# A four-layer graph network on one core: the fourth layer's neighbour weights applied before the sums

## The reference

```
h  = relu(layernorm(x));  x1 = x + log_softmax(sage(relu(sage(h))))        # layers 1 and 2
h  = relu(layernorm(x1)); h  = relu(mean(h)@W_l0.T + b_l0 + h@W_r0.T)      # layer 3: 128 -> 256
h  = relu(mean(h)@W_l1.T + b_l1 + h@W_r1.T)                                # layer 4: 256 -> 256
out = x1 + relu(h@W_lin1.T + b_lin1) @ W_lin2.T + b_lin2
```

## Time and profile before

| | |
|---|---|
| median of 3 runs | 591.04 us (590.75 to 591.55) |
| time of the profiled execution | 590.59 us |
| its span in the profile | 588.7 us |
| TensorE busy, matmuls / weight loads | 545.3 us (93%) / 291.9 us (50%) |
| VectorE, ScalarE, GpSimd busy | 223.0, 204.5, 24.0 us |
| granted TensorE clock, mean | 0.998 of full |
| DMA traffic | 29.47 MB, mean 50 GB/s |

### The profile page before, as it was taken

The page is one execution under the profiler, slowest core; times in us unless marked ns, Lnnn a source line. Parts: engine busy times, 40 slices in busy tenths (PEclk is TensorE's granted clock), DMA queues, the critical chain, the costliest instruction groups (busy, mean ns, idle before and its releaser), DMA issues.

```text
span 588.7 us, 9420 instructions
## 1 busy us (share of the span) xinstructions
PE 545.3 (93%) x3078; PEld 291.9 (50%) x3078; DVE 223.0 (38%) x496; ACT 204.5 (35%) x370; POOL 24.0 (4%) x34
## 2 busy tenths in 40 slices
PE   1356999999999999999999999999999999999996
PEld 0234655555554554445455555544545445454555
DVE  6788977586765316667511110100000001010001
ACT  1588867576774313545522221200001010100011
POOL 4320000000000000010100000000000000000000
PEclk9999999999999999999999999999999999999999
DMA  3700103010000134232131111241011211111011
GB/s 93 193 3 1 28 10 116 2 36 17 17 18 17 23 70 126 80 96 79 28 88 53 49 48 44 61 124 52 13 40 36 52 35 52 35 35 52 15 34 29
DMA packets 31372, 29.47 MB, mean 50 GB/s; under 512 B 4894, under 2 KB 30879, under 8 KB 31215
## 3 DMA queue, kind: packets, MB, share of 16 engines
q1 hardware_dynamic: 29622, 27.91, 17.1%
q10 hardware_dynamic: 1561, 0.84, 0.6%
q0 software_dynamic: 160, 0.33, 0.3%
HBM read 19.68 MB, written 9.39 MB: 49 GB/s over the span
## 4 chain that ended last, share of the span: by engine, by line
PE 86%; DVE 5%; ACT 3%; DMA 3%; issue 2%; POOL 1%; ACTq 0%; DVEq 0%; SPq 0%; POOLq 0%
PE ps L1025 54%; PE ps L1042 22%; PE ps L979 5%; PE ps L1297 2%; DVE hs_b L491 1%; DMA adj<-key_d,adj 1%; PE ps L1035 1%; ACT hs_b L796 1%; PE ps L1259 1%; ACT adj L1488 1%; DMA invc<-inv_d 1%; PE ps L1231 1%; DMA adj<-in_dst_dram 1%; POOL adj L1371 1%; DVE adj L1415 1%
## 5 line engine op out<-in xcount | busy, mean ns | idle before, releaser
L1025 PE MATMUL ps<-adj,hs_b 125*128 (+2 forms) x1050 | 203.6, 351 | 0.0
L1025 PE MATMUL ps<-adj,hs_a 125*128 (+2 forms) x700 | 158.4, 353 | 0.0
L1025 PEld LDWEIGHTS ps<-adj,hs_b 125*128 125x128 f16 x1050 | 96.3, 97 | 103.9 <-issue 6.6
L491 DVE TENSOR_TENSOR hs_b<-iota,hs_b 128x1024 f16<-128x1024 f16 x150 | 96.0, 688 | 29.4 <-PE ps L979 27.7
L979 PE MATMUL ps<-hs_b 128*128 128x125 f16 x625 | 69.4, 235 | 21.4 <-DVE hs_b L491 13.4
L835 ACT ACTIVATE adj<-ps 125x500 f32 (+2 forms) x150 | 80.2, 543 | 23.5 <-PE ps L979 17.0
L979 PEld LDWEIGHTS ps<-hs_b 128*128 128x128 f16 x625 | 46.7, 104 | 67.1 <-DVE hs_b L491 35.0
L1025 PEld LDWEIGHTS ps<-adj,hs_a 125*128 125x128 f16 x700 | 58.5, 97 | 38.7 <-issue 5.2
L964 ACT ACTIVATE actT<-ps,col 128x500 f32<-128x500 f32 (+1 forms) x14 | 8.9, 633 | 148.0 <-PE ps L1042 148.0
L785 DVE TENSOR_TENSOR hs_a<-ps,hs_a 125x512 f32<-125x512 f32 (+1 forms) x7 | 4.4, 635 | 128.5 <-PE ps L1297 128.5
L1042 PE MATMUL ps<-aggT,wts 128*128 128x500 f32 (+1 forms) x112 | 44.6, 540 | 0.4 <-ACT aggT L946 0.4
(11 more groups left out here) (149 smaller groups left out, 355.1 us busy)
## 6 DMA issues: line engine op xcount, KB each, us to landing
invc<-inv_d SPq DMA_DIRECT2D x24, 250.0 KB, 3.3
h_d<-actT SPq DMA_DIRECT2D x6, 500.0 KB, 3.1
wts<-h_d SPq DMA_DIRECT2D x6, 500.0 KB, 4.0
self_d<-hs_b SPq DMA_DIRECT2D x6, 250.0 KB, 2.0
hs_b<-self_d SPq DMA_DIRECT2D x6, 250.0 KB, 3.5
hs_b<-in_x_dram SPq DMA_DIRECT2D x6, 250.0 KB
x_d<-hs_b SPq DMA_DIRECT2D x6, 250.0 KB
hs_a<-x_d SPq DMA_DIRECT2D x6, 250.0 KB
```

The lines of the kernel that those rows point to most:

```text
L491: last = nc.vector.tensor_tensor(onehots[slot], iota2.unsqueeze(1).to_broadcast(shape), keys[:, ds(g * 4, 4), :].unsqueeze(2).to_broadcast ...
L1025: last = nc.tensor.matmul(acc[:, 0:n], hs[:, ds(s * (2 * w) + part * w + h * 128, 128)], adj[0:P, ds(c * (S * C) + s * n, n)], start=(isin ...
```

## The change

The rows of layer 4's input are multiplied by `Wl1` node by node before they are summed. `project3` takes the place of `turn3`: the block of `actT` that was transposed is now the stationary operand, and a 256 column half of `Wl1` moves. `own_term3` computes `Wr1` times the activations in layer 3; ScalarE adds the bias and sends that to DRAM (`v_d`) instead of the activations. In layer 4 `hidden4` is gone: VectorE scales the sum, adds `v`, and ScalarE applies the ReLU. As the projected rows need a scale, a bound is computed: four one-column matmuls in layer 2, step 1 (`bound_sums`), a small matmul (`bound_row`) in the last step, and on VectorE `projected_bound` and `projected_scale`, the latter ahead of layer 2's last `step2`. Two 256 KB weight loads are issued at the entry of layer 2. The branch for graphs that don't fit (`slow`) is changed alike and isn't run here. The diff, cut to its core:

```diff
@@ SyncE
             sp.wait_ge(sem("p1_low"), NCH)
             spread(2, hbz[:, 0:S * 2 * D], D, hs_d2)
+            sp.dma_start(wts[:, 512:1024], wt_d[:, 512:1024]).then_inc(sem("w1_in"), 16)
+            sp.dma_start(zT[:, 0:512], wt_d[:, 1024:1536]).then_inc(sem("w1_in"), 16)
...
-                sp.wait_ge(sem("p3_relu"), 2 * c + 2)
-                sp.dma_start(h3_d[:, :, ds(c * C, n)],
+                elif not slow:
+                    load_fourth()
+                n = width(full)
+                sp.wait_ge(sem("p3_vT"), 2 * c + 2)
+                sp.dma_start(v_d[:, :, ds(c * C, n)],
...
+            def load_fourth():
+                sp.wait_ge(sem("p3_agg_out"), NCH)
+                sp.wait_ge(sem("p3_own"), NCH)
+                sp.dma_start(w4, wt_d[:, 1536:2304]).then_inc(sem("w4_in"), 16)
+                load_inv("p4_", 0, True)
+                load_x1(0, True)
...
-                    sp.wait_ge(sem("p4_h4"), 2 * c + 2)
-                    load_h3(c + 1, nxt)
+                    sp.wait_ge(sem("p4_pre"), 2 * c + 2)
+                    load_v(c + 1, nxt)
@@ VectorE
+            def projected_bound():
+                dve.wait_ge(sem("u_bound"), 1)
+                lk(nc.vector.tensor_reduce(ubound, bank(6, 2), AX, ALU.max))
+                nc.vector.tensor_scalar(actT[:, 512:640], identf[:], 0.0, ubound, ALU.mult, ALU.add).then_inc(sem("u_spread"), 1)
+            def projected_scale():
+                dve.wait_ge(sem("u_bound"), 2)
+                lk(nc.vector.tensor_reduce(ubound, bank(0, 128), AX, ALU.max))
+                lk(nc.vector.tensor_scalar(ubound, ubound, TOP, None, ALU.mult))
+                pow2(lk, us, ius, ubound)
+                dve.sem_inc(sem("u_spread"), 1)
             step2(1, True)
+            projected_bound()
             with dve.Fori(2, NFULL) as c:
                 step2(c, True)
+            if not slow:
+                projected_scale()
             step2(NFULL, False)
...
-                    nc.vector.tensor_tensor(aggT[:, h * C:h * C + n], bank(h, n), invc[:, 0:n], ALU.mult).then_inc(
+                    nc.vector.scalar_tensor_tensor(o4, bank(h, n), ius, invc[:, 0:n], ALU.mult, ALU.mult).then_inc(
                         sem("p4_agg_out"), 1)
+                    dve.wait_ge(sem("p4_v"), 16 * c + 16)
+                    nc.vector.tensor_tensor(o4, o4, wts[:, h * C:h * C + n], ALU.add).then_inc(sem("p4_pre"), 1)
@@ ScalarE
+            act.wait_ge(sem("w1_in"), 32)
+            nc.scalar.activation(actT[:, 0:512], wts[:, 512:1024], ACT.Abs).then_inc(sem("abs_l1"), 1)
             chunks(act, step2)
...
+            def relu3(c, full):
+                wait_past(act, "p3_v_out", 16 * c)
...
+            def own_term(c, full):
+                act.wait_ge(sem("p3_v"), 2 * c + 2)
+                for m in range(2):
+                    nc.scalar.activation(actT[:, m * C:m * C + n], bank(4 + m, n), ACT.Identity,
+                                         bias=bl1c[:, m:m + 1]).then_inc(sem("p3_vT"), 1)
+            def step3(c, full):
+                high3(c - 1, True)
+                own_turned(c, full)
+                own_term(c - 1, True)
+                relu3(c, full)
@@ TensorE
+            def bound_sums():
+                for m in range(2):
+                    for k in range(2):
+                        last = nc.tensor.matmul(bank(6)[:, m:m + 1], actT[:, k * 256 + m * 128:k * 256 + m * 128 + 128], ones_c,
+                                                start=(k == 0), stop=(k == 1))
+            def bound_row():
+                nc.tensor.matmul(bank(0, 128), actT[:, 512:640], identf[:], start=True, stop=True)
+                   once=((1, 14, bound_sums), (NFULL, 12, bound_row)))
...
-                wait_past(pe, "p3_relu", 2 * c)
+                wait_past(pe, "p3_vT", 2 * c)
-            def turn3(c, full):
+            def project3(c, full):
                 pe.wait_ge(sem("p3_relu"), 2 * c + 2)
                 wait_past(pe, "p3_low", 2 * c)
...
-                            last = nc.tensor.transpose(bank(6 + k, 4 * D, P)[:, at:at + 128],
-                                                       actT[:, m * C + t * P:m * C + (t + 1) * P], identf[:])
+                            last = nc.tensor.matmul(bank(6 + k, 2 * H, P)[:, (t - t0) * H:(t - t0 + 1) * H],
+                                                    actT[:, m * C + t * P:m * C + (t + 1) * P], l1v[:, m, :],
+                                                    start=(m == 0), stop=(m == 1))
+            def own_term3(c, full):
+                pe.wait_ge(sem("p3_relu"), 2 * c + 2)
+                for m in range(2):
+                    dense(4 + m, n, [(r1v[:, k, m * 128:m * 128 + 128], actT[:, k * C:k * C + n]) for k in range(2)])
-            staged(3, [(lambda c: bank(acc3(c, slow)), ha, D, 0)], [(0, own3, 1), (8, hidden3, 1), (0, turn3, 2)],
+            staged(3, [(lambda c: bank(acc3(c, slow)), ha, D, 0)], [(0, own3, 1), (8, hidden3, 1), (0, project3, 2), (4, own_term3, 2)],
...
-                   [(10, hidden4, 1), (20, lin1, 1), (30, lin2, 1)],
-                   [(0, own3, NFULL), (0, turn3, NFULL - 1), (8, hidden3, NFULL), (16, turn3, NFULL)],
+                   [(7, lin1, 1), (17, lin2, 1)],
+                   [(0, own3, NFULL), (0, project3, NFULL - 1), (4, own_term3, NFULL - 1), (9, hidden3, NFULL),
+                    (15, project3, NFULL), (19, own_term3, NFULL)],
-                for part in (hidden4, lin1, lin2):
+                for part in (lin1, lin2):
                     part(NFULL, False)
```

More of the change, by code:

```diff
@@ L198, in sage_program @@
         mv = over(hs_b, up + 10368, 4 * 2, F32)[0:P]
[L200 removed]
+        w4 = over(hs_a, 0, 768, F32)
         x1in = over(hs_a, 7168, 4 * D, F32)[0:P]
@@ L432, in phase @@
                 if slow:
-                    pool.wait_ge(sem(f"p{ph}_rows"), 16)
+                    pool.wait_ge(sem("rows"), 16 * ph)
                 def step(c, full):
@@ L1154, in pe_layers @@
                 pe.wait_ge(sem("absw"), 2)
-                pe.wait_ge(sem("p1_rows"), 16)
+                pe.wait_ge(sem("rows"), 16)
                 chunks(pe, slow1)
@@ L1163, in pe_layers, with staged @@
                 step1(NFULL, False, None)
-            def staged(ph, aggs, parts, lead, source, fill=(0, 0)):
+            def staged(ph, aggs, parts, lead, source, fill=(0, 0), once=()):
                 def slow_step(c, full):
@@ L1212, in step @@
                                 part(c - lag, True)
+                        for of, tiles_done, part in once:
+                            if isinstance(c, int) and c == of and at == tiles_done:
+                                part()
                         if at % S == 0 and ph > 2 and at >= done:
@@ L1232, in turn2 @@
                 last.then_inc(sem("p2_turned"), 1)
+            def bound_sums():
+                pe.wait_ge(sem("abs_l1"), 1)
+                for m in range(2):
+                    for k in range(2):
+                        last = nc.tensor.matmul(bank(6)[:, m:m + 1], actT[:, k * 256 + m * 128:k * 256 + m * 128 + 128], ones_c,
+                                                start=(k == 0), stop=(k == 1))
+                last.then_inc(sem("u_bound"), 1)
+            def bound_row():
+                pe.wait_ge(sem("u_spread"), 1)
+                nc.tensor.matmul(bank(0, 128), actT[:, 512:640], identf[:], start=True, stop=True).then_inc(sem("u_bound"), 1)
+            if slow:
+                bound_sums()
             staged(2, [(each_own, hbz, D, 0)], [(7, turn2, 1)],
-                   [(0, own1, NFULL), (6, hidden1, NFULL), (12, second1, NFULL), (17, turn1, NFULL)], (NFULL - 1, NFULL, NCH))
+                   [(0, own1, NFULL), (6, hidden1, NFULL), (12, second1, NFULL), (17, turn1, NFULL)], (NFULL - 1, NFULL, NCH),
+                   once=((1, 14, bound_sums), (NFULL, 12, bound_row)))
+            if slow:
+                bound_row()
             pe.wait_ge(sem("w0_in"), 16)
@@ new lines, in project3 @@
+                    last.then_inc(sem("p3_u"), 1)
+            def own_term3(c, full):
+                n = width(full)
+                pe.wait_ge(sem("p3_relu"), 2 * c + 2)
+                for m in range(2):
+                    dense(4 + m, n, [(r1v[:, k, m * 128:m * 128 + 128], actT[:, k * C:k * C + n]) for k in range(2)]).then_inc(
+                        sem("p3_v"), 1)
+            staged(3, [(lambda c: bank(acc3(c, slow)), ha, D, 0)], [(0, own3, 1), (8, hidden3, 1), (0, project3, 2), (4, own_term3, 2)],
+                   [(14, turn2, NFULL)], (NFULL - 1, NFULL, NCH), fill=(5, 8))
@@ L1273, in hidden4, with lin1 @@
+            av = w4[:, 0:512].rearrange("p (k o) -> p k o", k=2)
+            bv = w4[:, 512:768].rearrange("p (k o) -> p k o", k=2)
+            def lin1(c, full):
                 n = width(full)
                 pe.wait_ge(sem("w4_in"), 16)
-                pe.wait_ge(sem("p4_h3"), 16 * c + 16)
-                pe.wait_ge(sem("p4_agg_out"), 2 * c + 2)
```

(7 more changed lines are left out.)

88 lines of the change are left out of this document (46 added, 42 removed).

## The result

The changed kernel takes **593.42 us** (591.80 to 594.82, 10 runs), the kernel before 590.76 (590.34 to 591.55, 10 runs). The ratio is 1.0044, with a 95% interval of 1.0033 to 1.0055, so 2.7 us more. The profiled execution took 594.35 with a span of 592.4 us, 3.7 more than before's 588.7.

A forecast was written before the change was run, and what follows sets the result against it. TensorE, 86% of the ending chain, was taken as the bound. Terms -5.3 + 0.2 + 0.6 + 1.75 - 0.15 + 1.1 + 0.9 + 1.45 + 0.2 = +0.75 us took the median from 591.04 to 591.8, range 589.6 to 594.4.

The forecast's parts named there:

- Full steps: Layers 3 and 4: steps of 21.2 us instead of 15.3, and 26.2 instead of 32.95.
- Rival B: Layer 3: `hidden3` waits in each step because ScalarE starts two evictions late; 593.6 us, chance 0.10.
- Matmul work: TensorE in layers 3 and 4: 47.8 us removed, 42.5 added, net -5.3 us.
- Rival D: Layer 3's projection: a 256 column instruction is paced by its weights, 0.233 us; 593.5 us, chance 0.07.
- Rival E: Layer 3: each removed transpose frees its recorded 0.279 us, 14.0 instead of 5.8; 583.6 us, chance 0.02.
- Short steps: Last steps of layers 3 and 4: chunk 5's `hidden3` +0.6 net, `lin1` +1.75, last `lin1` -0.15, v +0.2 us.
- The bound: Layer 2: one-column matmuls on TensorE +0.9 us, `projected_scale` on VectorE +1.45 us.
- The entry: Start of layer 2: two weight loads ahead of the inverse degrees cost +1.1 us, bounds 0 and 2.4.
- the two readings: Entry of layer 2: inverse degrees 0.6 us late, own term behind them 1.3 us late.
- the line: DMA landing time at layer 2's entry: 256 KB in 2.8 us, 896 KB in 5.8, 4.7 ns per KB.
- Rival A: Entry of layer 2: weight loads delay the inverse degrees by 2.4 us instead of 1.1; 593.1 us, chance 0.18.
- C: Entry of layer 2: the weight loads cost nothing, as x's data are the slow part; 590.7 us, chance 0.17.

The follow-up runs named there:

- the loads alone: Kernel before plus only the two weight loads at the entry of layer 2, data unused: 593.29 us, ratio 1.0039.
- loads early: Changed kernel with the two weight loads issued earlier, ahead of the entry of layer 2: 592.10 us, ratio 1.0018 to the kernel before.
- sums early: Changed kernel with the eight one-column matmuls ahead of tile 6 instead of tile 14 in layer 2: 592.43 us, ratio 1.0026 to the kernel before.
- no bound: Changed kernel with scale set to 1, bound computation left out, weight loads behind the entry's three loads: 589.71 us, ratio 0.9984 to the kernel before.
- all places: Changed kernel with weight loads and one-column matmuls earlier, scale last, `lin1` and `lin2` later, x1 load before output write: 588.48 us, ratio 0.9965 to kernel before.
- all in place: Changed kernel with all five placements mended, plus the short chunk's last sum written over its x1 rows: 588.54 us, ratio 0.9961 to the kernel before.
- the loads behind: Changed kernel with the two weight loads issued behind the three loads of layer 2's entry: 592.32 us, ratio 1.0021 to the kernel before.

## Why the prediction was partly right

The range, 589.6 to 594.4, held 593.42. The forecast itself, 591.8 and no difference that can be told (0.51), did not come true: the change is slower, which had 0.39, and 593.42 lies above the forecast's own range of 590.6 to 593.0. That the wide range held is partly luck, as its upper end was made of other terms than those that came. Step by step:

- **Full steps: right.** Layer 3 of 21.2 us and layer 4 of 26.24 were measured, and neither `hidden3` nor `lin1` waits in a full step. Rival B (ScalarE late) falls with the 118.86 us of the stretch to the short own rows, which every profile with the projection repeats (118.75 to 118.86).
- **Matmul work: right, slightly low.** The 256 column instruction takes 3.51/16 = 0.219 us, not 0.216: 0.35 us in all. Rival D (0.233) falls. Rival E falls too: the transposes gave back their pace, not their recorded length, as the +30.27 and -32.53 add up with 0.116 us each.
- **Short steps: right.** `lin1` of chunk 5 lost 1.75 by forecast, and the group ended at 575.28 + 3.59 = 578.87; the tiles ahead of it ended at 573.82, and with 3.35 behind them it would have been 577.17 without a wait: 1.7. The last `lin1` starts 1.15 us after the last tile, as worked out. `hidden3` of chunk 5 lost 1.2 (forecast 1.3). The wait for v was 0.36 (forecast 0.2).
- **The bound: right.** 0.96 us for the one-column matmuls and 1.5 for the scale were isolated, against 0.9 and 1.45.
- **The entry: the step that was sized too low.** I took +1.1 us "between the two readings", and 1.64 was measured (1.5 with the loads alone). The readings were themselves off: by the line 1012 KB land after 6.35 us, not 6.7, so the own term would be 1.0 late and not 1.3, and both readings lie below 1.1. Nor did the own term decide. The inverse degrees did: they landed at 217.83 + 5.29 = 223.12, 6.15 us behind the first load's issue at 216.97, where the line gave 5.2 us, 0.6 late. The line had no term for SyncE, which issues them 0.86 us behind the first load; the other 0.79 is their own slower landing. Rival A had 2.4 us for it, too much. But the test set for A was this operation starting more than 1.0 late, and it was 1.64 late: by that test A had come true. C, in which the loads cost nothing, falls.
- **The clock: a step that was missing.** The sum treated TensorE's wait as lost time only. Behind the wait of 2.11 us the profile shows the granted clock at half, 1.7 us more. With the 0.45 of layer 1, the 3.7 us of span are accounted for: 0.45 + 1.64 + 2.45 + 1.7 - 2.54. But by the mean clocks this happened in the profiled execution and in at most two more of the ten.

Without the half clock the terms give +1.5 us, 0.8 more than forecast, and most of that is the entry. The seven executions of after that leave no room for it are 2.4 us above before. So 0.9 us of the loss is in no stretch behind layer 1 of any profile, and its cause stays open. It isn't special to the change: the kernel before with the loads alone moved by 1.0 us more than its stretches say, and five kernels made from after (loads early, sums early, no bound, all places, all in place) by 0.5 to 0.7 more, but the one with the loads behind by nothing. The first 80 us, in which `adj` is built, were 0.5 us or more shorter in the one profile of before than in nine of the twelve others. They may hold part of it; one profile of before can't tell.

## What to carry to other kernels

Where a change moves work off the bound engine, price what it puts at the boundaries of the stages as carefully as the steady steps: here 2.5 us of gain in two layers met 4.1 us at the entry of another layer and inside it, and moving five items by a few lines turned a loss of 0.44% into a gain of 0.35%. The two loads put ahead of a DMA that was already on the ending chain cost 1.5 us and more, and 0.25 when they were issued earlier; look for such a place, and check that its reader isn't then in front of something else on its own engine. When a wait is removed near the end, look at which buffers come free later because of it: here two successive DMA waits took most of the 1.4 us.
